# Sixteen list entries per turn in four groups, on five accumulator slots, in an adjacency-and-tree kernel

## The reference

```python
def _L0_ffn_ref(x, w1s, b1s, w2s, b2s):
    DEPTH = 7
...
    current = jnp.zeros((T,), dtype=jnp.int32)
...
    for _ in range(DEPTH + 1):
        all_nodes.append(current)
        score = jnp.einsum('td,td->t', flat_x, w1s[current]) + b1s[current]
        all_logits.append(score)
        choice = ((jnp.sign(score) + 1.0) / 2.0).astype(jnp.int32)
        current = current * 2 + choice + 1
...
    path_weights = jax.nn.gelu(jnp.abs(logits), approximate=False)
...
    for i in range(DEPTH + 1):
        nodes_i = all_nodes[i]
        t_i = jnp.einsum('td,tdo->to', flat_x, w2s[nodes_i]) + b2s[nodes_i]
        out = out + t_i * path_weights[:, i][:, None]
...
    x = x + _L0_gnn_ref(_layernorm(x, axis=-1), L0_gnn_h_neigh, adj, adj, L0_gnn_Wq, L0_gnn_bq, L0_gnn_Wk, L0_gnn_bk, L0_gnn_Wv, L0_gnn_bv, L0_gnn_Wo, L0_gnn_bo, L0_gnn_E)
    x = x + _L0_ffn_ref(_layernorm(x, axis=-1)[None], L0_ffn_w1s, L0_ffn_b1s, L0_ffn_w2s, L0_ffn_b2s)[0]
```

## Time and profile before

| what | before |
|---|---|
| median of 3 runs | 167.42 us (167.17 to 168.17) |
| span of the profiled execution | 165.2 us |
| TensorE busy | 101.6 us (62%) |
| VectorE busy | 112.1 us (68%) |
| ScalarE busy | 69.9 us (42%) |
| GpSimd busy | 43.1 us (26%) |
| mean granted TensorE clock | 0.888 |

### The profile page before, as it was taken

The page is one execution under the profiler, slowest core; times in us unless marked ns, Lnnn a source line. Parts: engine busy times, 40 slices in busy tenths (PEclk is TensorE's granted clock), DMA queues, the critical chain, the costliest instruction groups (busy, mean ns, idle before and its releaser), DMA issues.

```text
span 165.2 us, 3073 instructions
## 1 busy us (share of the span) xinstructions
PE 101.6 (62%) x829; PEld 77.8 (47%) x830; DVE 112.1 (68%) x302; ACT 69.9 (42%) x167; POOL 43.1 (26%) x82
## 2 busy tenths in 40 slices
PE   0675007943878777865615444978888838688820
PEld 0161003833745555544504233537787738588720
DVE  0596904881699999996587689843645695846571
ACT  3232204890789989987100000335434322413420
POOL 2332920000000000000064000543443533754652
PEclk9999999997899999999755555599999999959996
DMA  5927640224999999999320000010000000000000
GB/s 155 306 81 207 115 105 25 50 74 141 383 405 446 421 440 436 412 442 406 156 65 0 0 4 0 16 48 0 0 4 4 0 2 0 16 16 0 0 6 26
DMA packets 6341, 22.35 MB, mean 135 GB/s; under 512 B 1755, under 2 KB 4826, under 8 KB 5722
## 3 DMA queue, kind: packets, MB, share of 16 engines
q1 hardware_dynamic: 4970, 20.78, 33.3%
q10 hardware_dynamic: 1104, 0.92, 1.8%
q0 software_dynamic: 256, 0.52, 1.1%
HBM read 20.91 MB, written 1.31 MB: 135 GB/s over the span
## 4 chain that ended last, share of the span: by engine, by line
PE 37%; DVE 17%; DMA 13%; issue 12%; ACT 9%; SPq 6%; POOL 2%; DVEq 1%; ACTq 0%; POOLq 0%
PE s_ps L641 11%; DMA early<-q_parts 7%; SPq L248 6%; PE turn_ps L641 4%; ACT prob L395 4%; PE turn_ps L512 3%; DVE prob L751 3%; ACT prob_t L391 3%; DVE row_pair L682 2%; DMA w_sb<-in_w_t 2%; PE aux_ps L641 2%; PE s_ps L566 2%; PE s_ps L539 2%; DMA q_parts<-q_p 2%; PE misc_ps L641 2%
## 5 line engine op out<-in xcount | busy, mean ns | idle before, releaser
L512 PE MATMUL turn_ps<-ident,prob 128*128 128x128 f32 x128 | 23.0, 309 | 8.0 <-ACT prob L395 6.6
L395 ACT ACTIVATE prob<-prob,negmax 128x512 f32<-128x512 f32 x32 | 23.0, 720 | 11.1 <-DVE negmax L751 11.0
L751 DVE CUSTOM_DVE_ANT_0 prob<-s_ps,mask 128x512 f32<-128x512 f32 x32 | 21.7, 682 | 8.5 <-PE s_ps L481 8.4
L353 POOL TENSOR_TENSOR early<-early,scaled_sb 128x128 f32<-128x128 f32 x48 | 20.5, 454 | 26.5 <-ACT scaled_sb L437 25.8
L758 DVE TENSOR_TENSOR prob_t<-turn_ps,prob_t 128x512 f16<-128x512 f32 x32 | 22.1, 689 | 6.2 <-ACT prob_t L391 6.2
L641 PE MATMUL s_ps<-w,msg 128*128 x128 | 19.2, 295 | 8.3 <-issue 4.5
L512 PEld LDWEIGHTS turn_ps<-ident,prob 128*128 128x128 f32 x128 | 15.8, 156 | 16.3 <-ACT prob L395 15.5
L481 PE MATMUL s_ps<-early 96*128 96x512 bf16 x32 | 13.7, 436 | 15.1 <-DMA early<-q_parts 14.2
L641 PEld LDWEIGHTS s_ps<-w,msg 128*128 128x128 f32 x128 | 16.3, 200 | 10.8 <-issue 10.7
L391 ACT ACTIVATE prob_t<-turn_ps 128x512 f16<-128x512 f32 x32 | 18.6, 580 | 6.6 <-PE s_ps L491 6.1
L437 ACT ACTIVATE scaled_sb<-s_ps,coef 128x128 f32<-128x128 f32 x32 | 10.0, 363 | 21.2 <-PE s_ps L641 21.2
(11 more groups left out here) (147 smaller groups left out, 163.8 us busy)
## 6 DMA issues: line engine op xcount, KB each, us to landing
w<-in_w_t SPq DMA_DIRECT2D x3, 4096.0 KB, 23.2
w<-in_w_t SPq DMA_DIRECT2D x1, 4032.0 KB, 41.6
prob<-in_adj SPq DMA_DIRECT2D x1, 1024.0 KB, 8.8
k_parts<-early SPq DMA_DIRECT2D x1, 384.0 KB, 2.5
early<-k_parts SPq DMA_DIRECT2D x1, 384.0 KB, 4.5
q_parts<-q_p SPq DMA_DIRECT2D x1, 288.0 KB, 3.4
early<-q_parts SPq DMA_DIRECT2D x1, 288.0 KB
msg<-in_neigh_t SPq DMA_DIRECT2D x1, 256.0 KB, 2.8
```

Source lines behind the costliest of these rows:

```text
L353: ins = nc.gpsimd.tensor_tensor(mine, mine, scaled_sb[:, i, :], ALU.add)
L395: nc.scalar.activation(prob[:, u % RING, :], prob[:, u % RING, :], ACT.Exp, bias=negmax[:, t, h:h + 1], scale=-1.0, accum_out=psums[:, t, ...
L512: last = nc.tensor.transpose(turn_ps[u % 2][:, m * P:(m + 1) * P], prob[:, u % RING, m * P:(m + 1) * P], ident[:])
L751: nc.vector.tensor_tensor_reduce(out=prob[:, u % RING, :], in0=score_ps[u % 2], in1=mask[:, t, :], scale=1.0, scalar=3.0e38, op0=ALU.add, ...
```

## The change

A turn now handles STEP = 16 entries in four groups (TURNS = 4), 0 and 2 on the four banks of `s_ps`, 1 and 3 on the other four. There are as many banks as before. `before_in_bank` names the group that used a group's banks last: group 2 waits for group 0 of the same turn, group 3 for group 1, groups 0 and 1 for 2 and 3 of the turn before. The lists are rounded up to a multiple of 16, by the same lines as before.

The accumulators are no longer one per entry: VectorE uses the slots 0 to 2 for all groups, ScalarE and GpSimd the slots 3 and 4. Since each group adds to the same slots as the one before it, VectorE and GpSimd wait at each group for their own previous group (`turn_before`). `acc` has five slots and the biases' sixth, and the reductions go over six. `scaled_sb` has six slots instead of three. GpSimd's loop no longer names the list.

```diff
--- before.py
+++ after.py
@@ -32,10 +32,13 @@
 RING = 4
 W2_PARTS = 4
 HALF = 4
-STEP = 2 * HALF
+TURNS = 4
+STEP = TURNS * HALF
 BY_DVE = (2, 3)
-BY_ACT = STEP - sum(BY_DVE)
-SUMS = STEP
+BY_ACT = tuple(HALF - n for n in BY_DVE)
+SCALED = sum(BY_ACT) * TURNS // 2
+DVE_SUMS = max(BY_DVE)
+SUMS = DVE_SUMS + max(BY_ACT)
 
 
 SUMMED_AFTER = ((), (0, 1), (2,), (3,))
@@ -74,14 +77,14 @@
     return lengths
 
 
-def tile_turns(nc, eng, lengths, nodes, turn, after):
+def tile_turns(nc, eng, lengths, nodes, turn, after, listed=True):
 
 
     start = STEP
     for s in range(TILES):
         end = eng.snap(lengths[s] + start)
         with eng.Fori(start, end, STEP) as e:
-            turn(s, list_entries(nc, eng.engine, nodes, e - start + s * NODES_PAD), e)
+            turn(s, list_entries(nc, eng.engine, nodes, e - start + s * NODES_PAD) if listed else None, e)
         after(s, end)
         start = end
 
@@ -154,7 +157,7 @@
         from_tile = sb("from_tile", [P, TILES, TILES + 1], F16)
         coef = sb("coef", [P, TILES, NODES_PAD])
         turned_up = sb("turned_up", [1, TILES], I32)
-        scaled_sb = sb("scaled_sb", [P, BY_ACT, D])
+        scaled_sb = sb("scaled_sb", [P, SCALED, D])
         active_h = sb("active_h", [P, 2, TILES], F16)
         active = sb("active", [P, 2 * TILES])
         rank = sb("rank", [P, 2 * TILES])
@@ -232,7 +235,7 @@
             sem("x1_sorted"), sem("biased"), sem("bias_moved"), sem("acc_zero"))
 
         multiplied, multiplied_last, added, scaled, pooled = (
-            [sem(f"{what}{half}") for half in range(2)]
+            [sem(f"{what}{g}") for g in range(TURNS)]
             for what in ("multiplied", "multiplied_last", "added", "scaled", "pooled"))
         tile_done, stored = sem("tile_done"), sem("stored")
 
@@ -247,10 +250,18 @@
                     rows = rows.unsqueeze(0).to_broadcast([times, n * DH, HEADS, hi - lo])
                 eng.dma_start(dst[r * DH:(r + n * times) * DH, :, lo:hi], rows).then_inc(stacked, 16)
 
-        def by_act(half):
-
-            first = (HALF - BY_DVE[0]) * half
-            return [(first + j - BY_DVE[half], j) for j in range(BY_DVE[half], HALF)]
+        def by_act(g):
+
+            first = sum(BY_ACT[i % 2] for i in range(g))
+            return [(first + j - BY_DVE[g % 2], j) for j in range(BY_DVE[g % 2], HALF)]
+
+        def before_in_bank(g, e):
+
+            return (g - 2, e + STEP) if g >= 2 else (g + 2, e)
+
+        def turn_before(g, e):
+
+            return (g - 1, e + STEP) if g >= 1 else (TURNS - 1, e)
 
         @block.sync
         def _(sp):
@@ -332,8 +343,8 @@
                 pool.wait_ge(q_stacked[i], 16 * len(Q_RUNS))
             pool.wait_ge(k_out, 16)
             nc.gpsimd.memset(acc[:, 1:SUMS], 0.0).then_inc(acc_zero, 1)
-            for half in range(2):
-                pool.sem_inc(pooled[half], STEP)
+            for g in range(TURNS):
+                pool.sem_inc(pooled[g], STEP)
 
             pool.wait_ge(x1_out, 16)
             pool.wait_ge(tokens_moved, 1)
@@ -345,13 +356,14 @@
             pool.wait_ge(acc_zero, 1)
 
             def add_scaled(s, found, e):
-                for half in range(2):
-                    pool.wait_ge(scaled[half], e + STEP)
-                    pool.wait_ge(pooled[half], e)
-                    for i, j in by_act(half):
-                        mine = acc[:, half * HALF + j, s, :]
+                for g in range(TURNS):
+                    pool.wait_ge(scaled[g], e + STEP)
+                    last, count = turn_before(g, e)
+                    pool.wait_ge(pooled[last], count)
+                    for i, j in by_act(g):
+                        mine = acc[:, DVE_SUMS + j - BY_DVE[g % 2], s, :]
                         ins = nc.gpsimd.tensor_tensor(mine, mine, scaled_sb[:, i, :], ALU.add)
-                    ins.then_inc(pooled[half], STEP)
+                    ins.then_inc(pooled[g], STEP)
 
             def store(s, end):
 
@@ -361,7 +373,7 @@
                         ap=token_s[:, tile:tile + 1], axis=0), in_=result[:, tile, :], in_offset=None
                                                  ).then_inc(stored, 16)
 
-            tile_turns(nc, pool, list_lengths(nc, pool.engine, entries), nodes, add_scaled, store)
+            tile_turns(nc, pool, list_lengths(nc, pool.engine, entries), nodes, add_scaled, store, listed=False)
             pool.wait_ge(stored, 16 * TILES)
 
         @block.scalar
@@ -426,17 +438,17 @@
                 nc.scalar.activation(coef_t[:, c, :], (turn_ps[1], misc_ps)[c][:], ACT.Copy
                                      ).then_inc(coef_t_ready, 1)
 
-            for half in range(2):
-                act.sem_inc(scaled[half], STEP)
+            for g in range(TURNS):
+                act.sem_inc(scaled[g], STEP)
 
             def scale(s, found, e):
-                for half in range(2):
-                    act.wait_ge(multiplied_last[half], e)
-                    act.wait_ge(pooled[half], e)
-                    for i, j in by_act(half):
-                        ins = nc.scalar.activation(scaled_sb[:, i, :], product_ps[half][j], ACT.Copy,
-                                                   scale=coef[:, s, bass.ds(found[HALF * half + j], 1)])
-                    ins.then_inc(scaled[half], STEP)
+                for g in range(TURNS):
+                    act.wait_ge(multiplied_last[g], e)
+                    act.wait_ge(pooled[g], e)
+                    for i, j in by_act(g):
+                        ins = nc.scalar.activation(scaled_sb[:, i, :], product_ps[g % 2][j], ACT.Copy,
+                                                   scale=coef[:, s, bass.ds(found[HALF * g + j], 1)])
+                    ins.then_inc(scaled[g], STEP)
 
             def move_biases(s, end):
                 if s < len(GROUPS):
@@ -628,25 +640,27 @@
 
 
             def products(s, found, e):
-                for half in range(2):
-                    pe.wait_ge(added[half], e)
-                    if (s, half) == (0, 1):
+                for g in range(TURNS):
+                    half = g % 2
+                    last, count = before_in_bank(g, e)
+                    pe.wait_ge(added[last], count)
+                    if (s, g) == (0, 1):
                         pe.wait_ge(coef_t_ready, 2)
-                    if half == 1 and 1 <= s <= len(GROUPS):
+                    if g == 1 and 1 <= s <= len(GROUPS):
                         pe.wait_ge(bias_moved, s)
                     for j in range(HALF):
                         if j == BY_DVE[half]:
-                            ins.then_inc(multiplied[half], STEP)
-                            pe.wait_ge(scaled[half], e)
+                            ins.then_inc(multiplied[g], STEP)
+                            pe.wait_ge(scaled[last], count)
                         ins = nc.tensor.matmul(product_ps[half][j], hs_t[:, s * P:(s + 1) * P],
-                                               w2[:, bass.ds(found[HALF * half + j], 1), :
+                                               w2[:, bass.ds(found[HALF * g + j], 1), :
                                                   ].rearrange("p n o -> p (n o)"), start=True, stop=True)
-                    ins.then_inc(multiplied_last[half], STEP)
+                    ins.then_inc(multiplied_last[g], STEP)
 
             def biases(s, end):
 
                 if s < len(GROUPS):
-                    pe.wait_ge(scaled[1], end)
+                    pe.wait_ge(scaled[TURNS - 1], end)
                     for tile in range(*GROUPS[s]):
                         for c in range(2):
                             last = nc.tensor.matmul(misc_ps[:, tile * D:(tile + 1) * D],
@@ -694,8 +708,8 @@
                         at += 1
                         dve.wait_ge(done, at)
 
-            for half in range(2):
-                dve.sem_inc(added[half], STEP)
+            for g in range(TURNS):
+                dve.sem_inc(added[g], STEP)
             dve.wait_ge(neigh_in, 16)
             dve.wait_ge(col_in, 16)
 
@@ -876,22 +890,22 @@
             lengths = list_lengths(nc, dve.engine, entries)
 
             def add_up(s, found, e):
-                for half in range(2):
-                    dve.wait_ge(multiplied[half], e)
-                    dve.wait_ge(added[half], e)
-                    for j in range(BY_DVE[half]):
-                        mine = acc[:, half * HALF + j, s, :]
+                for g in range(TURNS):
+                    dve.wait_ge(multiplied[g], e)
+                    last, count = turn_before(g, e)
+                    dve.wait_ge(added[last], count)
+                    for j in range(BY_DVE[g % 2]):
+                        mine = acc[:, j, s, :]
                         ins = nc.vector.scalar_tensor_tensor(
-                            out=mine, in0=product_ps[half][j], scalar=coef[:, s, bass.ds(found[HALF * half + j], 1)],
+                            out=mine, in0=product_ps[g % 2][j], scalar=coef[:, s, bass.ds(found[HALF * g + j], 1)],
```

(7 more changed lines are left out.)

## The result

| | before | changed |
|---|---|---|
| median | 167.79 us | 171.25 us (170.88 to 171.60) |
| ratio | | 1.0191, 95% interval 1.015 to 1.0232 |
| profiled span | 165.2 us | 169.8 us |
| first product to the end of the last reduction | 49.35 us | 52.89 us |

The account below looks back on a forecast made before the run. In the loop of products, TensorE's array works 1.78 of each 2.31 us turn, the rest being the loop itself. The new schedule summed to +0.28 us: 165.5 of span, plus 2.2 to the median, 167.7; range 165.2 to 170.2.

Parts of the forecast that it names:

- The turns and the padding: Loop of products: nine loops in place of sixteen, 144 products instead of 128; the 16 padding products 3.5 us of array.
- The wait for the banks: Turn starting at T: group 3 waits for VectorE's additions on group 1, starting at T + 2.96 instead of T + 2.64.
- the wait for the own group: VectorE's wait for its own previous group: up to about 0.13 per group, covered in the steady turn.
- the saved branch and load: Turn of 16: they come back as the bank wait; period 4.63 against 2 x 2.31 = 4.62, before the longer load.
- The load: TensorE's load of 16 list entries per turn: 0.14 longer than the 0.592 for eight, making the period 4.77.
- B, C and D: Loop stages ending at tile 1's bias products, tile 2's reduction and the last reduction's start: forecast 10.59, 12.47, 15.07.
- stage A: Loop from the first product to the bias products behind tile 0: forecast 9.93.
- Rival C: TensorE's load of 16 costs in proportion, 1.18 in all, on the path in six turns: +2.7, 170.4 us; chance 0.14.
- The reductions: Four reductions over six slots instead of nine: 1.43 instead of 2.11, all waited for, 2.7 us of relief.
- The clock: Tile 3: about 1.45 us lost to the 1.2 GHz level before; forecast kept the clock full after the change.

Follow-up runs that it names:

- e1: The kernel before, turns of eight, with lists rounded up to a multiple of 16 (18 turns instead of 16): 171.6 us, ratio 1.0183.
- e8: The changed kernel with eight accumulator slots again and no wait for the group just before: median 174.18 us, ratio 1.027.
- e5: The changed kernel with VectorE taking two banks of groups 1 and 3 instead of three, four accumulator slots: 170.1 us, ratio 1.0103.
- e4: The changed kernel with two loads of eight entries per turn instead of one of 16: 167.58 us, ratio 0.9975.
- e3: The changed kernel with two groups per turn: eight entries, lists rounded to eight, five accumulator slots kept: 164.33 us, ratio 0.9806.
- e0: The kernel before, unchanged, profiled once more: one execution, 169.81 us.
- e7: As e3 (eight entries per turn, shared slots), but VectorE takes two banks of each group, four slots: 163.65 us, ratio 0.9754.
- e2_load9: The kernel before, each turn of eight loading nine entries and using eight: one execution, 169.07 us.

## Why the prediction was wrong

**The turns and the padding: right.** Nine loops, 144 products, one more turn's worth in tiles 1 and 2 each. e1 has 2.32 and 2.34 us for them.

**The wait for the banks: right in place, and nearly in size.** Group 3 started at T + 3.07 where 2.96 was forecast; 0.09 of the difference is the wait for the own group, which the forecast took as covered in a steady turn (e8, where it is gone, has T + 2.98). It was held by VectorE's additions on group 1, and the sequencer's lead was lost. e5 took the wait away and group 3 started at T + 2.66. The claim that the saved branch and load come back as this wait holds: with loads of eight (e4) two turns' work takes 4.83, against 2 x 2.31.

**The load: wrong, and this is the miss.** The step was: "0.07 for four more, so 0.14 for eight more as an estimate". It was 0.51. I drew a line through two rows, 0.523 for four and 0.592 for eight, of which the first was another load from another tensor; above eight the load has steps of 0.256 for four entries. Then "I take 0.14 since TensorE's own rows are nearest" closed the range at the value that should have been doubted: the rows ended at eight, and the change went to 16. e4 shows it: with loads of eight B, C and D follow the forecast's schedule and add up to 38.40 instead of the changed kernel's 40.78, and the ratio falls by 0.0216, 3.6 us. So 2.4 us of the load are seen in these three stages. The other 1.2, itself within the intervals of the two ratios, would lie in stage A and ahead of the loop, and there the profiles don't separate it: A has a turn of 3.34 in the changed kernel (115.87 to 119.21, the longer load), but 10.74 in e4 too, since the first turn there took 3.22 instead of 2.56. The same long first turn stands in e1 and e3 (3.43 and 3.18), and not in e0 or e7 (2.77 and 2.72), so it goes with neither the load nor the slots. It goes with VectorE's start: where the first turn takes over 3 us, VectorE begins to load the list lengths 0.9 to 1.2 after its memset of `coef` (1.01 in e4, 1.24 in e1, 0.98 in e3), elsewhere 0.2 to 0.6 after it (0.31 before, 0.27 in the changed kernel); why is open. So it is in part luck that e4's median of 167.58 meets the forecast: in its profile the loop is 1.1 longer than forecast and begins 1.3 earlier. Rival C had this mechanism and, with 0.45 extra per turn, 170.4 us; measured was 0.37 and 171.25. I gave it 0.14 of the chance against the row from four to eight.

Two pages of the Trainium skill bear on this load. The Trainium skill, Runtime: NRT & Kernel Launch (Instruction fetch mechanics), has about 200 ns per register. It speaks of loads from HBM, a condition that the prediction left out; the measured 1.105 for 16 is 69 ns each, so the figure can't be carried over to these loads from SBUF. The Trainium skill, DMA: Bandwidth & Descriptors (Latency and other measured facts), gives a floor of about 600 ns for a `tensor_load`. TensorE's 0.592 for eight lies at it, its 0.523 for four and ScalarE's 0.548 for eight somewhat below it; how the load grows above the floor the page doesn't say.

**The reductions: size right, worth too high.** 1.48 against 1.43. But "There are four, all with somebody waiting: 4 x 0.68 = 2.7 us of relief" forgot that VectorE, once late, now pays for its own waits, which I had counted only for the first group behind a reduction. In turns of eight its load of list entries comes into the open with them (0.60 in e3). e8 puts the slots at 1.3 us in the changed kernel by the ratios, with an interval wider than that, and at 1.75 by the loop.

**The clock: right for the changed kernel, less sure for the one before.** It stayed full in the loop of the changed kernel. The sum also took 1.45 us as gained back, from one profile of the kernel before; e0 has a fall too, but in another place and of 2.1 us, and how much of it the median holds isn't known.

In one sum, by ratios at 167.7 us: the slots -3.3 (e3), the padding +3.1 (e1), the four groups themselves -0.2 (e4 against the product of both, 0.9975 against 0.9985, far inside the intervals), the load of 16 +3.6 (changed against e4, 1.0191 against 0.9975). Three terms of nearly one size, two up and one down. Their intervals are 1.0 us on either side for the slots, 1.6 for the padding and about 1 for the load, so the sizes are rough and only the signs are firm. And the first two are measured against a kernel that loses time to its clock in both its profiles: by the stages of the loop without such a fall, the padding costs 4.66 and the slots of e3 gain 0.7.

## What to carry to other kernels

Before you make a loop larger to save its overhead, price what grows with it: here, by the ratios, the padding took 3.1 us and the longer register load 3.6, while what was saved came back as a wait for banks. Where a price is read from rows at one size and the change goes to twice that size, the upper end of the range is at least proportional growth; better, split the load so that the size stays that of a known row, and put the second one where the sequencer is ahead. And take the parts of a change apart: the shorter accumulators, alone with small turns, were the whole gain (0.9806, and 0.9754 with the work shared 2 to 2).

## What the runs showed of the hardware

- A load of list entries from SBUF into TensorE's registers took 0.592 us for 8, 0.844 for 9, 0.849 for 12 and 1.105 for 16. VectorE's took 0.599, 0.843, 0.850 and 1.10, ScalarE's 0.548, 0.776, 0.782 and 1.02.
- VectorE's load of the next turn ran under a reduction (at 135.0, reduction to 135.83) where the additions of the turn could all be issued ahead, and in the open (at 136.7, last addition to 136.56) where one group had to be done before the next could be issued.
- When TensorE's sequencer is held by a wait in the last group of a turn, the array pauses later, at the start of the next turn, and the pause is put down to "issue" (1.14 in e5), not to the engine that was waited for.
- TensorE's clock fell to the 1.2 GHz level behind pauses of 2.69 and 1.89 us in two profiles of the same kernel, each time behind only one of them, and behind neither 2.64 nor 1.79 in e1 and neither 2.43 nor 1.72 in e2_load9.
